# Ternary convolution after group norm: Newton step of the norm's scale on GpSimd, with the planes and copies of image 1 rearranged

## The chip, the cores and the metric

The kernel runs on one core of a Trainium2 chip. Its engines are TensorE (PE in the rows), VectorE (DVE), ScalarE (ACT), GpSimd (POOL) and SyncE (SP, which issues transfers here). The metric is the device time of the one launch, in microseconds. "Before" is the kernel as it was, "after" the changed one.

## The reference

x is 32 images of 128 channels, 56 x 56, float32. Each image is normalized in 32 groups of 4 channels, convolved 3 x 3 with ternary weights, and added to the input.

```python
def reference(x, weight, bias, Wp, Wn):
    g = x.reshape(32, 32, 4, 56, 56)
    m = mean(g, axis=(2, 3, 4)); s = var(g, axis=(2, 3, 4))
    xn = ((g - m) / sqrt(s + 1e-5)).reshape(x.shape)
    w = weight / max(abs(weight)); delta = 0.05 * max(abs(w))
    tern = where(w > delta, 1, where(w < -delta, -1, 0))
    wq = where(tern > 0, Wp * tern, where(tern < 0, Wn * tern, tern))
    return x + conv3x3(xn, wq, padding=1) + bias
```

## The kernel before

**Data.** Channels lie on the 128 partitions, and one image is one unit of work. The rows of an image are taken in pairs: two output rows are made from four products instead of six, so each image has four "planes" of 28 x 56 sums and differences of input rows, called C, D, A and B (`plane[j]`). A plane is scaled by `norm_scale` (256 over the standard deviation) and cut into a float16 high part and a float16 low part (`parts`). TensorE multiplies both parts with the three columns of the turned weights: `multiply`, 24 matmuls for each plane, 96 for an image. Products C and A go to the even output rows' PSUM tile, D and B to the odd rows'.

**Slots.** Each engine runs its own program and follows the same sequence of slots (`slots`): in one slot it works on images `prev`, `now`, `nxt` and `far` (the images k-1, k, k+1, k+2). Slots at both ends are written out, those between run in a loop of four. The engines are tied only by semaphores. What an engine does in a slot, and in which order, is its `emit`. There are 33 slots; the first has no `now`, in the second `now` is image 0, in the third `now` is image 1.

**One ordinary slot.** VectorE makes the low part of D (`make_lo`, L607), reads the variance of the next image out of PSUM (`variance`, L585), makes the low part of A, plane C of the next image (`make_c`, L561), its plane D (`make_d`, L567), then the reciprocal of its standard deviation (`first_rstd`, L591) and two more tiny instructions for the scale (`newton_factor`, L596, and `scale_of_x`, L602, one Newton step on the rough root), the low part of B, the next plane A (`make_a`, L573) and the next low part of C, and last evicts four half images of output rows out of PSUM (`output_rows`, L622). ScalarE makes the high parts (`make_hi`, L388), copies the finished products C and D out of PSUM with the bias (`copy_c`, L373, `copy_d`, L379), takes the square root (`root`, L440), and sums x and its squares two images ahead (L394, L434). GpSimd makes the next plane B (`difference_b`, L326), which waits for `lo_ready[C]` of the same image, and issues the two transfers that add the residual x to the output (`add_residual`, L339). SyncE loads images and stores outputs; each image has one of four buffers.

**TensorE's order in a slot** is product C, the group sum of squares of `nxt` (`sum_var`, L757, two tiny float32 matmuls), product D, product A, the group sum of `far` (`sum_mean`, L752), product B. Product C waits for `lo_ready[C]` and for the first half of the previous image's even rows; product D waits for `lo_ready[D]`; A for `lo_ready[A]` and `c_ready`; B for `lo_ready[B]` and `d_ready`.

**The scale's way.** `sumsq_ready` -> `sum_var` -> `variance` -> `root` (ScalarE) -> `first_rstd` -> Newton step -> `scale_of_x_ready`, for which ScalarE's `make_hi(nxt, C)` waits, and VectorE's `make_lo(nxt, C)` waits for that.

Of the kernel before, what the change touches and what calls it, by code (L numbers as in the profile page):

```python
# [6 lines left out]
P = 128  # L7
# [23 lines left out]
def conv_preact_kernel(nc, x, weight, bias, wp, wn, out):  # L31
# [15 lines left out]
    with ExitStack() as ctx:  # L47
        def sb(name, shape, dt=F32):
            return ctx.enter_context(nc.sbuf_tensor(name, shape, dt))
# [38 lines left out]
        rstd0 = sb("rstd0", [P, X_BUFS])  # L88
        newton = sb("newton", [P, X_BUFS])
        norm_scale = sb("norm_scale", [P, X_BUFS])  # L90
# [44 lines left out]
        newton_ready = sem("newton_ready")  # L135
# [164 lines left out]
        def _(pool):  # L300
# [19 lines left out]
            def run(p):  # L320
                def difference_b(img):
                    pool.wait_ge(x_loaded[img.buf], img.turn * 32 + 32)
                    wait(pool, lo_ready[B], img.count())
                    pool.wait_ge(lo_ready[C], img.count(plus=1))
                    even = x_sb[img.buf][:, 0:H:2, :]
                    nc.gpsimd.tensor_tensor(plane[B][:, 0:PAIRS - 1, :], even[:, 0:PAIRS - 1, :], even[:, 1:, :],  # L326
                                            ALU.subtract).then_inc(plane_ready[B], 1)
# [13 lines left out]
                def emit(prev, now, nxt, far):  # L341
                    if now and nxt:
                        difference_b(nxt)
                    if now and nxt:
                        add_residual(now, 0)
                        add_residual(now, 1)

                slots(p, pool, emit)

            run(0)  # L350
# [6 lines left out]
        def _(act):  # L357
# [8 lines left out]
            def run(p):  # L366
# [76 lines left out]
                def emit(prev, now, nxt, far):  # L443
# [20 lines left out]
                    elif now:  # L464
                        make_hi(now, A)
                        make_hi(now, B)
                        copy_c(now)
                        if nxt:
                            root(nxt)
                        if far:  # L470
                            sum_x(far)
                        copy_d(now)
                        if nxt:
                            make_hi(nxt, C)
# [22 lines left out]
        def _(dve):  # L497
            nc.vector.memset(no_bias[:], 0.0).then_inc(zero_ready, 1)
# [46 lines left out]
            def run(p):  # L545
# [47 lines left out]
                def newton_factor(img):  # L593
                    b = b_slice(img)
                    dve.wait_ge(rstd_ready, img.count(plus=1))
                    nc.vector.tensor_scalar(newton[:, b], rstd0[:, b], rstd0[:, b], neg_var[:, b],  # L596
                                            ALU.mult, ALU.mult).then_inc(newton_ready, 1)

                def scale_of_x(img):
                    b = b_slice(img)  # L600
                    dve.wait_ge(newton_ready, img.count(plus=1))
                    nc.vector.tensor_scalar(norm_scale[:, b], newton[:, b], 3.0, rstd0[:, b],  # L602
                                            ALU.add, ALU.mult).then_inc(scale_of_x_ready, 1)

# [42 lines left out]
                def emit(prev, now, nxt, far):  # L647
                    first_slot, second_slot = not now and not prev, now and not prev
                    if first_slot:
# [8 lines left out]
                        newton_factor(nxt)  # L658
                        scale_of_x(nxt)
                        turned_weights((C, D))  # L660
                        make_first_lo(nxt)
                    if second_slot:
# [10 lines left out]
                        newton_factor(nxt)  # L673
                        scale_of_x(nxt)
# [3 lines left out]
                    elif now:  # L678
                        third_slot = prev.j == 0 and prev.q == p * N_IMG // X_BUFS
                        make_lo(now, D)  # L680
                        if third_slot:
                            make_a(now)
# [3 lines left out]
                        if nxt:  # L686
                            make_c(nxt)
                            make_d(nxt)
                            first_rstd(nxt)
                            newton_factor(nxt)  # L690
                            scale_of_x(nxt)
# [174 lines left out]
```

## Time and profile before

| | |
|---|---|
| time, median of 3 runs | 567.59 us (567.28 to 568.82) |
| the profiled execution's own time | 566.68 us |
| its span in the trace | 565.0 us |
| busy: PE / DVE / ACT / POOL | 531.7 / 543.4 / 504.1 / 162.6 us |
| share of the span: PE / DVE / ACT / POOL | 94% / 96% / 89% / 29% |
| granted TensorE clock, mean | 0.996 of full speed |
| bytes moved, mean rate | 153.43 MB, 272 GB/s |

How to read it: busy times are sums over one profiled execution. The span is shorter than the execution's own time by 1.7 us, which lies outside the first and last instruction. Consecutive VectorE and ScalarE instructions overlap by some 0.1 us in the records, so the price of an instruction in a full queue is the distance from its start to the next start, not its duration.

### The profile page before, as it was taken

The page shows a single profiled execution, that of the slowest core. Times are in us where ns is not written, and L with a number is a line of the kernel's source. Part 1 is how long each engine was busy: PE and PEld are TensorE (multiplying, and loading weights), DVE is VectorE, ACT ScalarE, POOL GpSimd, SP SyncE. Part 2 cuts the span into 40 slices and gives each one's busy share as a digit, 9 for nine tenths or more (in the row PEclk, how much of TensorE's full clock was granted, in tenths as well). Part 3 has the DMA queues.
Part 4 walks back from the last instruction along what each step waited for, and adds up shares of the span by engine and source line. Part 5 has one row for each costly group of instructions (what it writes and reads, how often), then busy time and mean ns, then how long its engine had stood idle before and what let it go on. Part 6 is the DMA issues. An engine that isn't in the chain of part 4 may idle for free.

```text
span 565.0 us, 9357 instructions
## 1 busy us (share of the span) xinstructions
PE 531.7 (94%) x3233; PEld 319.3 (57%) x3233; DVE 543.4 (96%) x506; ACT 504.1 (89%) x485; POOL 162.6 (29%) x106
## 2 busy tenths in 40 slices
PE   1898999999999999999999999999999999999994
PEld 0654555655555555555555555556555555555552
DVE  4998999999999999999999999999999999999994
ACT  4898999999999999999999999999999999999850
POOL 2030333311333331233332123333113333312330
PEclk9999999999999999999999999999999999999998
DMA  8439799999999999999999999999999999998767
GB/s 295 202 115 256 239 286 293 293 261 266 289 299 288 313 278 270 294 294 318 297 297 278 279 298 261 309 282 302 268 301 277 292 289 304 293 281 195 155 180 276
DMA packets 28105, 153.43 MB, mean 272 GB/s; under 512 B 3505, under 2 KB 3505, under 8 KB 28081
## 3 DMA queue, kind: packets, MB, share of 16 engines
q1 hardware_dynamic: 18576, 102.77, 48.2%
q0 software_dynamic: 8928, 49.78, 45.5%
q10 hardware_dynamic: 576, 0.59, 0.3%
q8 instruction: 12, 0.20, 0.1%
q14 instruction: 13, 0.10, 0.0%
HBM read 101.75 MB, written 51.38 MB: 271 GB/s over the span
## 4 chain that ended last, share of the span: by engine, by line
DVE 69%; issue 23%; PE 2%; ACT 2%; DMA 1%; DVEq 1%; ACTq 0%
DVE parts L607 26%; DVE y L622 19%; DVE plane L561 10%; DVE plane L567 9%; DVE newton L596 2%; PE odd_rows L766 1%; DMA x<-in_x_dram 1%; DVE plane L573 1%; PE even_rows L766 1%; DVEq L157 1%; DVE neg_var L585 1%; ACT junk L434 1%; DVE rstd L591 0%; DVE parts L613 0%; ACT junk L394 0%
## 5 line engine op out<-in xcount | busy, mean ns | idle before, releaser
L766 PE MATMUL odd_rows<-parts,w_lhsT 128*128 128x385 f16 (+1 forms) x1536 | 266.1, 330 | 7.8 <-DVE parts L607 7.5
L766 PE MATMUL even_rows<-parts,w_lhsT 128*128 128x385 f16 (+1 forms) x1536 | 265.6, 330 | 3.6 <-ACT c_sb L373 2.3
L607 DVE SCALAR_TENSOR_TENSOR parts<-plane,norm_scale,parts 128x1568 f16<-128x1568 f32 x127 | 233.5, 1843 | 1.7 <-ACT parts L388 1.7
L326 POOL TENSOR_TENSOR plane<-x 128x1512 f32<-128x1512 f32 x31 | 105.8, 3412 | 379.1 <-DVE parts L607 379.1
L766 PEld LDWEIGHTS even_rows<-parts,w_lhsT 128*128 128x128 f16 x1536 | 149.3, 98 | 110.0 <-issue 4.9
L388 ACT ACTIVATE parts<-plane,norm_scale 128x1568 f16<-128x1568 f32 x127 | 199.9, 1597 | 11.8 <-ACT plane L428 5.2
L766 PEld LDWEIGHTS odd_rows<-parts,w_lhsT 128*128 128x128 f16 x1536 | 147.9, 99 | 107.3 <-DVE parts L607 9.8
L434 ACT ACTIVATE junk<-x,negmean 128x3136 f16<-128x3136 f32 x32 | 92.9, 2904 | 0.1
L394 ACT ACTIVATE junk<-x 128x3136 f16<-128x3136 f32 x31 | 86.9, 2804 | 0.0
L622 DVE SCALAR_TENSOR_TENSOR y<-even_rows,out_scale,d_sb 128x784 f32<-128x784 f32 x62 | 61.0, 1026 | 0.0
L622 DVE SCALAR_TENSOR_TENSOR y<-odd_rows,out_scale,c_sb 128x784 f32<-128x784 f32 x62 | 60.9, 1024 | 0.0
L561 DVE SCALAR_TENSOR_TENSOR plane<-x,neg2mean 128x1568 f32<-128x1568 f32 x32 | 59.0, 1845 | 0.0
L567 DVE TENSOR_TENSOR plane<-x 128x1568 f32<-128x1568 f32 x32 | 57.1, 1784 | 0.4 <-ACT junk L402 0.4
L379 ACT ACTIVATE d_sb<-odd_rows,bias_sb,out_scale 128x1568 f32<-128x1568 f32 x32 | 52.6, 1643 | 5.3 <-PE odd_rows L766 5.3
L573 DVE TENSOR_TENSOR plane<-x 128x1512 f32<-128x1512 f32 x32 | 55.2, 1725 | 0.0
L339 POOL DMA_DIRECT2D y<-in_x_dram x62 | 54.3, 887 | 3.2 <-DVE y L622 0.5
L373 ACT ACTIVATE c_sb<-even_rows,bias_sb,out_scale 128x1568 f32<-128x1568 f32 x32 | 52.5, 1641 | 0.5 <-DVE out_scale L543 0.4
L419 ACT ACTIVATE neg2mean<-odd_rows 128x1 f32<-128x1 f32 x32 | 5.4, 170 | 22.7 <-PE odd_rows L752 21.6
L757 PEld LDWEIGHTS odd_rows<-sums,group_mean 128*128 128x128 f32 x64 | 11.6, 194 | 5.6 <-issue 3.5
L752 PEld LDWEIGHTS odd_rows<-sums,group_mean 128*128 128x128 f32 x62 | 11.2, 195 | 3.4 <-DVE parts L607 0.9
L757 PE MATMUL odd_rows<-sums,group_mean 128*128 128x1 f32 x64 | 9.2, 213 | 3.4 <-ACT junk L434 3.4
L427 ACT ACTIVATE plane<-x,negmean 128x56 f32<-128x56 f32 x32 | 10.6, 332 | 0.0
(65 smaller groups left out, 109.9 us busy)
## 6 DMA issues: line engine op xcount, KB each, us to landing
x<-in_x_dram SPq DMA_DIRECT2D x64, 784.0 KB, 11.0
out_dram<-y SPq DMA_DIRECT2D x63, 784.0 KB, 5.6
y<-in_x_dram POOLq DMA_DIRECT2D x62, 784.0 KB, 11.9
out_dram<-y SPq DMA_DIRECT2D x2, 392.0 KB, 5.9
y<-in_L_conv_weight_dram ACTq DMA_DIRECT2D x1, 576.0 KB, 6.7
wp_sb<-in_L_conv_Wp_dram ACTq DMA_DIRECT2D x1, 0.5 KB, 7.7
wn_sb<-in_L_conv_Wn_dram ACTq DMA_DIRECT2D x1, 0.5 KB, 7.9
bias_sb<-in_L_conv_bias_dram ACTq DMA_DIRECT2D x1, 0.5 KB, 7.6
```

The source lines that it names most:

```text
L326: nc.gpsimd.tensor_tensor(plane[B][:, 0:PAIRS - 1, :], even[:, 0:PAIRS - 1, :], even[:, 1:, :], ALU.subtract).then_inc(plane_ready[B], 1)
L339: pool.dma_start(y, of, accum_op=ALU.add).then_inc(residual_added[img.buf][h], 16)
L379: nc.scalar.activation(d_sb[:], product_ps(ODD), ACT.Identity, bias=(no_bias if p else bias_sb)[:, 0:1], scale=out_scale[:, p, 1:2]).then_ ...
L388: nc.scalar.activation(part(img, j, HI), plane[j][:], ACT.Copy, scale=norm_scale[:, b_slice(img)]).then_inc(hi_ready[j], 1)
L394: nc.scalar.activation(junk[:], x_sb[img.buf][:].rearrange("p h w -> p (h w)"), ACT.Copy, accum_out=sums[:, img.buf, 1:2]).then_inc(sum_re ...
L434: nc.scalar.activation(junk[:], x_sb[img.buf][:].rearrange("p h w -> p (h w)"), ACT.Square, bias=negmean[:, b_slice(img)], accum_out=sums[ ...
L561: nc.vector.scalar_tensor_tensor(plane[C][:], xs[:, 0:H:2, :], neg2mean[:, b_slice(img)], xs[:, 1:H:2, :], ALU.add, ALU.add).then_inc(plan ...
L567: nc.vector.tensor_tensor(plane[D][:], xs[:, 1:H:2, :], xs[:, 0:H:2, :], ALU.subtract).then_inc(plane_ready[D], 1)
L573: nc.vector.tensor_tensor(plane[A][:, 1:, :], odd[:, 1:, :], odd[:, 0:PAIRS - 1, :], ALU.subtract).then_inc(plane_ready[A], 1)
L607: nc.vector.scalar_tensor_tensor(part(img, j, LO), plane[j][:], norm_scale[:, b_slice(img)], part(img, j, HI), ALU.mult, ALU.subtract).the ...
L622: nc.vector.scalar_tensor_tensor(rows_of(y_sb[img.buf], h, odd), product_ps(odd, 2 * h, 2 * h + 2), out_scale[:, p, 0:1], other[:, 2 * h:2 ...
L766: ins = nc.tensor.matmul(product_ps(odd, b, b + 1)[:, 0, :, to:to + n], w_lhsT[:, prod, kw, :], part(img, prod, which)[:, b * BANK_ROWS:(b ...
```

## The change

Three things. (1) VectorE loses `newton_factor` and `scale_of_x`; GpSimd does the same arithmetic in four instructions on 128 x 1 values, each waiting for the one before by a semaphore: square, times `neg_var`, plus three, times `rstd0`. It does so at the head of its slot, ahead of plane B and of the residual transfers. In VectorE's ordinary slots the reciprocal moves from behind `make_d` to ahead of it. (2) In the second slot GpSimd makes plane A of image 1 (`second_a`), ahead of plane B; VectorE no longer makes it in the third slot. (3) In the third slot ScalarE copies c ahead of the high parts of A and B instead of behind them. A tile `three` is filled once by VectorE. The diff runs through GpSimd's program first, then ScalarE's, then VectorE's.

```diff
+            def run(p):
+                def scale_of_x(img):
+                    b = b_slice(img)
+                    pool.wait_ge(rstd_ready, img.count(plus=1))
+                    nc.gpsimd.tensor_tensor(rstd_sq[:, b], rstd0[:, b], rstd0[:, b], ALU.mult).then_inc(newton_step, 1)
+                    pool.wait_ge(newton_step, img.count(3, 1))
+                    nc.gpsimd.tensor_tensor(less[:, b], rstd_sq[:, b], neg_var[:, b], ALU.mult).then_inc(newton_step, 1)
+                    pool.wait_ge(newton_step, img.count(3, 2))
+                    nc.gpsimd.tensor_tensor(newton[:, b], less[:, b], three[:], ALU.add).then_inc(newton_step, 1)
+                    pool.wait_ge(newton_step, img.count(3, 3))
+                    nc.gpsimd.tensor_tensor(norm_scale[:, b], newton[:, b], rstd0[:, b],
+                                            ALU.mult).then_inc(scale_of_x_ready, 1)
+                def second_a(img):
+                    pool.wait_ge(x_loaded[img.buf], img.turn * 32 + 32)
+                    wait(pool, lo_ready[A], img.count())
+                    odd = x_sb[img.buf][:, 1:H:2, :]
+                    nc.gpsimd.tensor_tensor(plane[A][:, 1:, :], odd[:, 1:, :], odd[:, 0:PAIRS - 1, :],
+                                            ALU.subtract).then_inc(plane_ready[A], 1)
...
                 def emit(prev, now, nxt, far):
+                    if nxt:
+                        scale_of_x(nxt)
+                    if now and not prev:
+                        second_a(nxt)
                     if now and nxt:
                         difference_b(nxt)
                     if now and nxt:
                         add_residual(now, 0)
                         add_residual(now, 1)
...
+            pool.wait_ge(zero_ready, 1)
             run(0)
...
                     elif now:
-                        make_hi(now, A)
-                        make_hi(now, B)
-                        copy_c(now)
+                        if prev.j == 0 and prev.q == p * N_IMG // X_BUFS:
+                            copy_c(now)
+                            make_hi(now, A)
+                            make_hi(now, B)
+                        else:
+                            make_hi(now, A)
+                            make_hi(now, B)
+                            copy_c(now)
...
+            nc.vector.memset(three[:], 3.0)
...
                     elif now:
-                        third_slot = prev.j == 0 and prev.q == p * N_IMG // X_BUFS
                         make_lo(now, D)
-                        if third_slot:
-                            make_a(now)
                         if nxt:
                             variance(nxt)
                         make_lo(now, A)
                         if nxt:
                             make_c(nxt)
+                            first_rstd(nxt)
                             make_d(nxt)
-                            first_rstd(nxt)
-                            newton_factor(nxt)
-                            scale_of_x(nxt)
                         make_lo(now, B)
```

In the first two slots VectorE's two calls go too, and its reciprocal stays where it was.

**VectorE, one ordinary slot.** The kernel before, from the low part of D to the first evictions (line numbers of before):

```order
L607 SCALAR_TENSOR_TENSOR parts<-plane,norm_scale,parts 128x1568
L585 TENSOR_SCALAR neg_var<-odd_rows 128x1
L607 SCALAR_TENSOR_TENSOR parts<-plane,norm_scale,parts 128x1568
L561 SCALAR_TENSOR_TENSOR plane<-x,neg2mean 128x1568
L567 TENSOR_TENSOR plane<-x 128x1568
L591 RECIPROCAL rstd<-std 128x1
L596 TENSOR_SCALAR newton<-rstd,neg_var 128x1
L602 TENSOR_SCALAR norm_scale<-newton,rstd 128x1
L607 SCALAR_TENSOR_TENSOR parts<-plane,norm_scale,parts 128x1568
L573 TENSOR_TENSOR plane<-x 128x1512
L607 SCALAR_TENSOR_TENSOR parts<-plane,norm_scale,parts 128x1568
L622 SCALAR_TENSOR_TENSOR y<-even_rows,out_scale,d_sb 128x14x56 x2
```

And the changed kernel at the same place (line numbers of after):

```order
L630 SCALAR_TENSOR_TENSOR parts<-plane,norm_scale,parts 128x1568
L620 TENSOR_SCALAR neg_var<-odd_rows 128x1
L630 SCALAR_TENSOR_TENSOR parts<-plane,norm_scale,parts 128x1568
L596 SCALAR_TENSOR_TENSOR plane<-x,neg2mean 128x1568
L626 RECIPROCAL rstd<-std 128x1
L602 TENSOR_TENSOR plane<-x 128x1568
L630 SCALAR_TENSOR_TENSOR parts<-plane,norm_scale,parts 128x1568
L608 TENSOR_TENSOR plane<-x 128x1512
L630 SCALAR_TENSOR_TENSOR parts<-plane,norm_scale,parts 128x1568
L645 SCALAR_TENSOR_TENSOR y<-even_rows,out_scale,d_sb 128x14x56 x2
```

The two tiny instructions are gone, and the reciprocal stands one large instruction earlier: three large ones (plane D, low part of B, plane A) now lie between it and the next low part of C.

**GpSimd, from the constants to the end of the second slot.** Before, after the constants (`turn`) the first work is plane B of image 1:

```order
L310 AFFINE_SELECT ident<-ident 128x128
L313 AFFINE_SELECT group_mean<-group_mean 128x128
L317 AFFINE_SELECT turn<-turn 128x128 x3
L326 TENSOR_TENSOR plane<-x 128x1512
L339 DMA y<-in_x_dram 128x1568 x2
```

In the changed kernel, for image 1 (the four tiny ones for image 0 stand once more ahead of these):

```order
L328 TENSOR_TENSOR rstd_sq<-rstd 128x1
L330 TENSOR_TENSOR less<-rstd_sq,neg_var 128x1
L332 TENSOR_TENSOR newton<-less,three 128x1
L334 TENSOR_TENSOR norm_scale<-newton,rstd 128x1
L342 TENSOR_TENSOR plane<-x 128x1512
L350 TENSOR_TENSOR plane<-x 128x1512
L363 DMA y<-in_x_dram 128x1568 x2
```

Each later slot has the same rows without L342, so plane B and the residual's transfers now stand behind four tiny instructions that wait for VectorE's reciprocal.

**ScalarE, third slot.** Before (the row at L388 is the high parts of A and B, L373 the copy of c):

```order
L388 ACTIVATE parts<-plane,norm_scale 128x1568 x2
L373 ACTIVATE c_sb<-even_rows,bias_sb,out_scale 128x1568
L440 ACTIVATE std<-neg_var 128x1
L394 ACTIVATE junk,sums<-x 128x3136
L379 ACTIVATE d_sb<-odd_rows,bias_sb,out_scale 128x1568
```

The changed kernel there:

```order
L402 ACTIVATE c_sb<-even_rows,bias_sb,out_scale 128x1568
L417 ACTIVATE parts<-plane,norm_scale 128x1568 x2
L469 ACTIVATE std<-neg_var 128x1
L423 ACTIVATE junk,sums<-x 128x3136
L408 ACTIVATE d_sb<-odd_rows,bias_sb,out_scale 128x1568
```

Only the copy of c moved, ahead of the two high parts; the later slots keep the old order.

## Rows read from the trace of the kernel before

**Rows 1.** The page's busy table: busy us, share of the span, instructions.

```profile
PE 531.7 (94%) x3233; PEld 319.3 (57%) x3233; DVE 543.4 (96%) x506; ACT 504.1 (89%) x485; POOL 162.6 (29%) x106
```

**Rows 2.** Timeline, VectorE, one slot: start us, duration us, line, operation.

```profile
260.97 1.84 DVE L607 SCALAR_TENSOR_TENSOR parts<-plane,norm_scale,parts 128x1568 f16<-128x1568 f32 x1
262.73 0.15 DVE L585 TENSOR_SCALAR neg_var<-odd_rows 128x1 f32<-128x1 f32 x1
262.80 1.84 DVE L607 SCALAR_TENSOR_TENSOR parts<-plane,norm_scale,parts 128x1568 f16<-128x1568 f32 x1
264.56 1.84 DVE L561 SCALAR_TENSOR_TENSOR plane<-x,neg2mean 128x1568 f32<-128x1568 f32 x1
266.32 1.78 DVE L567 TENSOR_TENSOR plane<-x 128x1568 f32<-128x1568 f32 x1
268.02 0.15 DVE L591 RECIPROCAL rstd<-std 128x1 f32<-128x1 f32 x1
268.22 0.27 DVE L596 TENSOR_SCALAR newton<-rstd,neg_var 128x1 f32<-128x1 f32 x1
268.52 0.21 DVE L602 TENSOR_SCALAR norm_scale<-newton,rstd 128x1 f32<-128x1 f32 x1
268.65 1.84 DVE L607 SCALAR_TENSOR_TENSOR parts<-plane,norm_scale,parts 128x1568 f16<-128x1568 f32 x1
270.41 1.73 DVE L573 TENSOR_TENSOR plane<-x 128x1512 f32<-128x1512 f32 x1
272.06 1.84 DVE L607 SCALAR_TENSOR_TENSOR parts<-plane,norm_scale,parts 128x1568 f16<-128x1568 f32 x1
```

**Rows 3.** Chain that ended last: first and last plane C of the ordinary slots.

```profile
65.16 1.85 DVE plane L561
...
530.43 1.85 DVE plane L561
```

**Rows 4.** Timeline, TensorE, the same slot; [idle before <-releaser].

```profile
258.36 4.15 PE L766 MATMUL even_rows<-parts,w_lhsT 128*128 128x392 f16 x24
262.35 0.28 PE L757 MATMUL odd_rows<-sums,group_mean 128*128 128x1 f32 x2
262.87 4.16 PE L766 MATMUL odd_rows<-parts,w_lhsT 128*128 128x392 f16 x24 [0.24 <-DVE parts L607]
266.87 4.15 PE L766 MATMUL even_rows<-parts,w_lhsT 128*128 128x392 f16 x24
270.86 0.28 PE L752 MATMUL odd_rows<-sums,group_mean 128*128 128x1 f32 x2
271.00 4.15 PE L766 MATMUL odd_rows<-parts,w_lhsT 128*128 128x392 f16 x24
```

**Rows 5.** Timeline, ScalarE, same slot: next high part of C, next mean.

```profile
268.86 1.59 ACT L388 ACTIVATE parts<-plane,norm_scale 128x1568 f16<-128x1568 f32 x1
271.17 0.17 ACT L419 ACTIVATE neg2mean<-odd_rows 128x1 f32<-128x1 f32 x1 [0.72 <-PE odd_rows L752]
```

**Rows 6.** GpSimd's groups by form: count, busy us, mean ns, idle before.

```profile
L326 POOL TENSOR_TENSOR plane<-x 128x1512 f32<-128x1512 f32 x31 | 105.8, 3412 | 379.1 <-DVE parts L607 379.1
...
L308 POOL TENSOR_SCALAR_AFFINE_SELECT group_mean<-group_mean 128x128 f32<-128x128 f32 x1 | 0.5, 518 | 0.1
...
L855 POOL MEMSET const-float32-0.0<- 128x1 f32 x1 | 0.1, 98 | 0.4 <-issue 0.4
```

**Rows 7.** Timeline, the first and the third slot, ScalarE, TensorE and VectorE.

```profile
19.20 1.77 ACT L413 ACTIVATE parts<-plane,norm_scale 128x784 f16<-128x784 f32 x2
...
43.37 0.28 PE L757 MATMUL odd_rows<-sums,group_mean 128*128 128x1 f32 x2
...
45.13 3.10 ACT L388 ACTIVATE parts<-plane,norm_scale 128x1568 f16<-128x1568 f32 x2 [1.98 <-DVE plane L573]
46.77 1.85 DVE L607 SCALAR_TENSOR_TENSOR parts<-plane,norm_scale,parts 128x1568 f16<-128x1568 f32 x1 [1.65 <-ACT parts L388]
```

**Rows 8.** The page's DMA issues: count, KB each, median us to landing.

```profile
x<-in_x_dram SPq DMA_DIRECT2D x64, 784.0 KB, 11.0
```

More of the change, by code:

```diff
@@ L88, in conv_preact_kernel @@
         rstd0 = sb("rstd0", [P, X_BUFS])
+        rstd_sq = sb("rstd_sq", [P, X_BUFS])
+        less = sb("less", [P, X_BUFS])
         newton = sb("newton", [P, X_BUFS])
+        three = sb("three", [P, 1])
         norm_scale = sb("norm_scale", [P, X_BUFS])
@@ L134, in conv_preact_kernel @@
         rstd_ready = sem("rstd_ready")
-        newton_ready = sem("newton_ready")
+        newton_step = sem("newton_step")
         scale_of_x_ready = sem("scale_of_x_ready")
@@ L591, in first_rstd @@
                     nc.vector.reciprocal(rstd0[:, b], std[:, b]).then_inc(rstd_ready, 1)
[L593 to L603, printed above, removed]
                 def make_lo(img, j):
@@ L672, in emit @@
                         first_rstd(nxt)
-                        newton_factor(nxt)
-                        scale_of_x(nxt)
                         make_lo(now, B)
@@ L687, in emit @@
                             make_c(nxt)
+                            first_rstd(nxt)
                             make_d(nxt)
-                            first_rstd(nxt)
-                            newton_factor(nxt)
-                            scale_of_x(nxt)
                         make_lo(now, B)
```

## The prediction

> **What bounds the kernel now.** I read the busy table first: VectorE is at 96% [rows 1]. That is an average, so I then read the chain that ended last, which is a string of VectorE instructions, one image after another: plane C starts at 65.16 and, 28 slots on, at 530.43 [rows 3], so a slot takes 465.27 / 28 = 16.617 us. The timeline of one slot shows why: VectorE's starts follow each other with no gap [rows 2]. TensorE is close behind. Product C starts at 258.36, the sum of squares at 262.35 (3.99 later), product D at 262.87, A at 266.87, the group sum at 270.86 and B at 271.00 [rows 4]. A group sum that nobody holds up costs 0.14 (270.86 to 271.00); the one before D costs 0.52, because D waits for its low part. So TensorE loses only 0.38 us in a slot, and could do one in 16.617 - 0.38 = 16.24. ScalarE waits 0.72 for the next mean [rows 5], so it isn't the bound either. GpSimd makes one plane in 3.41 us and is idle for 379.1 us in all [rows 6].
>
> **VectorE's part of the change.** From the reciprocal's start to the next large instruction are 268.65 - 268.02 = 0.63 us [rows 2]. A tiny instruction that nothing waits on costs about 0.07 (262.73 to 262.80, the variance), so the reciprocal alone will cost 0.07, and each slot gets 0.56 us shorter on VectorE: 16.06. The root must be there earlier now, at plane C's end (266.32). It is made from the variance at 262.73, and ScalarE has it well before its copy of d and the high part at 268.86; I charge nothing.
>
> **What stops TensorE next.** VectorE cannot simply run at 16.06, and the slot does not fall to 16.24 either. VectorE takes the variance only after TensorE's sum of squares: 0.28 us after its start (its duration) at least, 0.38 at most (262.35 to 262.73) [rows 2, 4]; I take 0.33. From there VectorE needs a slot of its own, 16.06, plus 0.08 for the end of the next low part of D (260.97 + 1.84 = 262.81 against 262.73), and 0.06 to release product D: D starts 16.53 after the previous sum of squares. From D's start to the next sum of squares TensorE needs 4.00 + 3.99 + 0.14 + 3.98 + 3.99 = 16.10. This chain (sum of squares, VectorE's slot, product D, TensorE's slot) spans two images: 32.63 / 2 = 16.31 us (16.29 to 16.34 with 0.28 and 0.38). It is longer than TensorE's own 16.24 and VectorE's own 16.06, so it is the new bound: 0.307 saved in each of 28 slots, **8.6 us**.
>
> **GpSimd's chain.** The trace of before has no tiny two-input instruction on GpSimd. Bounds from its rows: not less than the 0.10 of a 128 x 1 fill, and hardly more than the 0.52 of a select over 128 x 128 floats [rows 6]; with some 0.1 for each semaphore hand-over the four cost 0.8 to 2.5 us. I take 0.2 + 0.1 each, 1.2 us in all, nearer to the fill because the size is the fill's. The cover: the reciprocal will end 0.15 after plane C, the low part of C starts after plane D, the low part of B and plane A, 1.70 + 1.76 + 1.65 = 5.11 less 0.08, and ScalarE's high part must lie before it (1.59, and 0.05 for the hand-over): **3.4 us** are free [rows 2, 5]. Against ScalarE's own time the cover is also enough at 1.2: in before's clock the reciprocal ends near 266.5 and the scale is there at 267.7, ScalarE comes at 268.86. If that cover fails, every further microsecond falls on VectorE's low part of C in each slot. Queued behind the four on GpSimd are plane B, which waits for that low part anyway, and the residual's two transfers, issued after the evictions: nothing later for them. Their head start on the next reciprocal is several us.
>
> **Transfers.** Loads take 11.0 us to land [rows 8] and are issued four images ahead into the freed buffer, over 30 us before their first reader; the whole saving over all slots, about 10 us, is less than that slack, so even a transfer rate that cannot grow costs nothing.
>
> **The edges.** Third slot: ScalarE is free at 45.13 - 1.98 = 43.15 and waits for VectorE's plane A; VectorE then waits 1.65 for the high part until 46.77 [rows 7]. After the change plane A comes from GpSimd in the second slot. If GpSimd starts it behind its tiny chain at about 33 it ends at 36.7, and plane B, released near 37.2 by the low part of C, at 40.7, both before 43.15. ScalarE copies c when product C is done (43.37), for 1.54, makes the high part of A from 44.96 to 46.55, and VectorE's low part starts at 46.6 instead of 46.77: only 0.1, since the copy now stands in front; with the 0.56 of this slot 0.7. What TensorE gains earlier in that slot is lost again, because its next product C waits for VectorE's evictions. Second slot: VectorE gains 0.56, but the next image's sum of x on ScalarE sets the slot, so nothing. First slot: the scale comes 0.70 us after the reciprocal's start now and 0.15 + 1.2 = 1.35 then; ScalarE starts its first high part at 19.20 without a wait, so between 0 and 0.65 is lost; I take 0.1. Last slots: the last pass through VectorE's chain once more, 0.56 less what it now waits, about 0.4.
>
> **The sum**, against the profiled execution's own 566.68: 8.6 + 0.7 + 0.4 - 0.1 = 9.6, so 557.1. The median of the runs shown is 0.9 higher, so I forecast **558.0 us**.
>
> **Rivals.**
> (a) *GpSimd and VectorE take turns, and the scale comes late: slower.* All of VectorE's large instructions behind the reciprocal read two SBUF tensors, and so do the new GpSimd ones. In before no such pair ever overlaps: plane B waits for the low part of C in all 31 cases (379.1 us of idle time) and lies beside the evictions, which read PSUM and one SBUF tensor [rows 6]. So the trace neither shows nor excludes it. If a GpSimd instruction has to wait for the end of VectorE's current one, the first gets in behind plane D, the second behind the low part of B, the third behind plane A, and the fourth when VectorE stands at the low part of C. Then 0.3 for the fourth, 1.64 for the high part: VectorE waits about 2.0 in each slot, and each of the first three lets it wait some 0.1 more. 16.06 + 2.0 + 0.3 = 18.4, 1.75 more than now, times 29 slots is +51: **about 618 us** (610 to 628). It decides from the point where the chain of four takes over 3.4 + 0.56 = 4.0 us: then VectorE waits at the low part of C for as long as it saved. For it speaks that the wait on the low part of C is no data dependence, which leaves plane B clear of exactly these instructions; against it, that reading a value of 128 x 1 is over at once, so that the gap of some 0.1 between two large instructions may do. The Trainium skill (SBUF — State Buffer, Who interferes with whom) says that a VectorE instruction with two SBUF inputs contends with a GpSimd instruction that reads SBUF, and that the side that comes first holds the shared ports. By that rule the time would be that of this rival; no run here shows it yet. Chance 0.17.
> (b) *The same contention, but mild:* GpSimd's instructions slip in, and each holds VectorE for 0.1 to 0.15. Four give VectorE's slot 16.06 + 0.4 to 0.6, that is 16.46 to 16.66, against 16.617 now: 561.5 to 568.5. Chance 0.12.
> (c) *No gain:* TensorE or ScalarE turns out to run no faster than 16.6 for a reason that its idle time hides. Against it, TensorE has the 0.38 and ScalarE 0.72. 566 to 569. Chance 0.06.
> (d) *A GpSimd instruction of this form simply takes over 0.9 us*, without any contention; the chain, with 0.1 for each hand-over, then passes 4.0 us. At 1.2 each it is 4.8, and the slot 16.06 + 1.4 = 17.5, +24: 592. All rows of small GpSimd work stand at 0.1 to 0.5 against it. Chance 0.03.
> The forecast itself (chain hidden, new bound at 16.31): 0.62.
>
> **How the numbers follow.** Low end: TensorE at its own 16.24 would save 0.38 x 28 = 10.6 instead of 8.6, and the edges up to 0.7 more, which is 555.3; 554.5 with the spread of runs. High end: (b) and (c), 568.5. What lies outside is (a) and (d), 0.20. A measurement of this kernel tells 0.3%, 1.7 us, from no change. Faster: the forecast 0.62 and less than half of (b), 0.05, in all 0.67. Same: (c) 0.06 and most of the rest of (b), 0.07, together 0.13. Slower: 0.20.
>
> **What would show it.** Right: plane C to plane C 16.31 on average, with alternating long and short slots possible; a wait of VectorE for the sum of squares at the variance (0.1 to 0.3) where none was; TensorE's wait at D down from 0.24; GpSimd's four instructions done within 1.2 us of the reciprocal, and no wait of ScalarE for the scale; in the third slot the low part of A released at 46.6. Wrong: tiny GpSimd instructions that start only where a large VectorE instruction ends; ScalarE's high part of C waiting for GpSimd, and VectorE's low part of C for ScalarE; large VectorE instructions with gaps of 0.1 and more between their starts.

## The result, and the profile after

The changed kernel takes **628.14 us** (median of 4 runs, 627.01 to 630.18), before 567.43 (4 runs): ratio 1.107, interval 1.105 to 1.110. It is 60.7 us slower. The forecast was 558.0; rival (a), that GpSimd and VectorE take turns and the scale comes late, had been given 618 and a chance of 0.17.

The busy table of the page, after, against [rows 1]:

```profile
PE 541.1 (86%) x3233; PEld 317.3 (51%) x3233; DVE 530.5 (85%) x442; ACT 503.6 (80%) x485; POOL 331.4 (53%) x235
```

Nobody is at 96% any more: VectorE lost 13 us of work and is now idle for 96 us of 626, and GpSimd doubled its busy time, though it got only 128 instructions on 128 x 1 values and one plane. Its groups say which (count, busy us, mean ns; behind the second bar the idle time before them and what ended it), to be read against [rows 6]:

```profile
L350 POOL TENSOR_TENSOR plane<-x 128x1512 f32<-128x1512 f32 x31 | 105.8, 3413 | 112.8 <-DVE parts L630 112.8
L330 POOL TENSOR_TENSOR less<-rstd_sq,neg_var 128x1 f32<-128x1 f32 x32 | 100.1, 3130 | 2.5
...
L328 POOL TENSOR_TENSOR rstd_sq<-rstd 128x1 f32<-128x1 f32 x32 | 53.3, 1665 | 152.6 <-DVE rstd L626 152.6
L334 POOL TENSOR_TENSOR norm_scale<-newton,rstd 128x1 f32<-128x1 f32 x32 | 6.1, 189 | 2.5
L332 POOL TENSOR_TENSOR newton<-less,three 128x1 f32<-128x1 f32 x32 | 6.1, 189 | 2.5
```

Four instructions of one form and one size take 1665, 3130, 189 and 189 ns on average. The size can't be the reason; what stands beside them can. The timeline of the changed kernel (start us, duration us, engine, line; in brackets the idle time before and what ended it), first in the opening slots, then in one ordinary slot:

```profile
17.95 1.00 DVE L586 CAST w_lhsT<-even_rows 128x384 f16<-128x384 f32 x2
18.18 0.19 POOL L328 TENSOR_TENSOR rstd_sq<-rstd 128x1 f32<-128x1 f32 x1 [14.49 <-DVE rstd L626]
...
21.38 5.87 PE L780 MATMUL even_rows<-parts,w_lhsT 128*128 128x392 f16 x24 [0.65 <-DVE parts L636]
...
33.52 3.43 POOL L328 TENSOR_TENSOR rstd_sq<-rstd 128x1 f32<-128x1 f32 x1 [14.33 <-DVE rstd L626]
...
37.70 3.40 POOL L342 TENSOR_TENSOR plane<-x 128x1512 f32<-128x1512 f32 x1
...
39.42 3.33 DVE L630 SCALAR_TENSOR_TENSOR parts<-plane,norm_scale,parts 128x1568 f16<-128x1568 f32 x1 [2.53 <-ACT parts L417]
...
45.08 5.98 PE L780 MATMUL even_rows<-parts,w_lhsT 128*128 128x392 f16 x24
...
54.42 1.85 DVE L630 SCALAR_TENSOR_TENSOR parts<-plane,norm_scale,parts 128x1568 f16<-128x1568 f32 x1 [3.04 <-ACT parts L417]
...
278.76 0.16 DVE L626 RECIPROCAL rstd<-std 128x1 f32<-128x1 f32 x1
278.83 1.77 DVE L602 TENSOR_TENSOR plane<-x 128x1568 f32<-128x1568 f32 x1
279.00 1.66 POOL L328 TENSOR_TENSOR rstd_sq<-rstd 128x1 f32<-128x1 f32 x1 [3.93 <-DVE rstd L626]
...
280.52 1.85 DVE L630 SCALAR_TENSOR_TENSOR parts<-plane,norm_scale,parts 128x1568 f16<-128x1568 f32 x1
280.74 3.33 POOL L330 TENSOR_TENSOR less<-rstd_sq,neg_var 128x1 f32<-128x1 f32 x1
282.28 1.73 DVE L608 TENSOR_TENSOR plane<-x 128x1512 f32<-128x1512 f32 x1
...
284.14 0.19 POOL L332 TENSOR_TENSOR newton<-less,three 128x1 f32<-128x1 f32 x1
284.41 0.19 POOL L334 TENSOR_TENSOR norm_scale<-newton,rstd 128x1 f32<-128x1 f32 x1
284.63 1.60 ACT L417 ACTIVATE parts<-plane,norm_scale 128x1568 f16<-128x1568 f32 x1 [2.58 <-POOL norm_scale L334]
...
286.26 1.85 DVE L630 SCALAR_TENSOR_TENSOR parts<-plane,norm_scale,parts 128x1568 f16<-128x1568 f32 x1 [2.25 <-ACT parts L417]
```

Read it by where things end. In the ordinary slot plane D ends at 278.83 + 1.77 = 280.60, and GpSimd's first tiny instruction at 280.66. Plane A ends at 284.01, the second tiny one at 284.07. Once VectorE has run out of work, the third and fourth take 0.19 each, 0.27 from start to start. Then ScalarE makes the high part, and VectorE, which stood at the low part of C since about 283.92, starts it at 286.26: 2.3 us lost in each slot. VectorE's own instructions are not stretched: from plane D to the low part of B it takes 1.69 and on to plane A 1.76, as in [rows 2] (1.70 with the reciprocal behind it, and 1.76). At 18.18, beside a VectorE instruction that reads PSUM, the same GpSimd instruction takes 0.19.

Where the 61.6 us between the two profiled executions (628.3 and 566.68) lie:

| stretch | before | after | more |
|---|---|---|---|
| start to the fourth plane C, the first counted in [rows 3] | 65.16 | 74.58 | 9.4 |
| 28 slots, plane C to plane C | 465.27 (16.617 each) | 515.11 (18.397 each) | 49.8 |
| last plane C to the end of the span | 34.57 | 36.51 | 1.9 |
| outside the span | 1.7 | 2.1 | 0.4 |

### The profile page after: what moved, and what is told of

Read it like the earlier page. It is cut to its first block, busy times and chain, and to the rows that moved or that the text cites. A ratio compares the mean times of both kernels' runs of the same rounds, so it can differ in the third digit from the quotient of the medians.

```text
span 626.2 us, 9501 instructions
## 1 busy us (share of the span) xinstructions
PE 541.1 (86%) x3233; PEld 317.3 (51%) x3233; DVE 530.5 (85%) x442; ACT 503.6 (80%) x485; POOL 331.4 (53%) x235
## 4 chain that ended last, share of the span: by engine, by line
POOL 40%; issue 25%; DVE 16%; ACT 10%; PE 5%; POOLq 2%; DMA 1%; DVEq 0%; ACTq 0%
POOL less L330 16%; DVE parts L630 10%; POOL plane L350 10%; POOL rstd_sq L328 8%; ACT parts L417 8%; DVE y L645 4%; POOL y L363 4%; PE even_rows L780 2%; PE odd_rows L780 2%; DMA x<-in_x_dram 1%; POOL newton L332 1%; POOL norm_scale L334 1%; DVE plane L596 1%; ACT junk L423 1%; POOLq L363 0%
## 5 line engine op out<-in xcount | busy, mean ns | idle before, releaser
L780 PE MATMUL even_rows<-parts,w_lhsT 128*128 128x385 f16 (+1 forms) x1536 | 269.4, 333 | 49.0 <-DVE y L645 46.8
L417 ACT ACTIVATE parts<-plane,norm_scale 128x1568 f16<-128x1568 f32 x127 | 200.0, 1598 | 90.4 <-POOL norm_scale L334 82.4
L780 PEld LDWEIGHTS odd_rows<-parts,w_lhsT 128*128 128x128 f16 x1536 | 146.0, 100 | 112.1 <-DVE parts L630 11.1
L328 POOL TENSOR_TENSOR rstd_sq<-rstd 128x1 f32<-128x1 f32 x32 | 53.3, 1665 | 152.6 <-DVE rstd L626 152.6
L330 POOL TENSOR_TENSOR less<-rstd_sq,neg_var 128x1 f32<-128x1 f32 x32 | 100.1, 3130 | 2.5
L608 DVE TENSOR_TENSOR plane<-x 128x1512 f32<-128x1512 f32 x31 | 53.7, 1732 | 0.0
```

What stands on the lines that cost most here:

```text
L328: nc.gpsimd.tensor_tensor(rstd_sq[:, b], rstd0[:, b], rstd0[:, b], ALU.mult).then_inc(newton_step, 1)
L330: nc.gpsimd.tensor_tensor(less[:, b], rstd_sq[:, b], neg_var[:, b], ALU.mult).then_inc(newton_step, 1)
L417: nc.scalar.activation(part(img, j, HI), plane[j][:], ACT.Copy, scale=norm_scale[:, b_slice(img)]).then_inc(hi_ready[j], 1)
L780: ins = nc.tensor.matmul(product_ps(odd, b, b + 1)[:, 0, :, to:to + n], w_lhsT[:, prod, kw, :], part(img, prod, which)[:, b * BANK_ROWS:(b ...
```

## The experiments

Nine more kernels ran. Most of them test a theory T against a rival R. Theory T: while VectorE runs an instruction with two SBUF inputs, a GpSimd instruction that reads SBUF waits. Rival R: the long tiny instructions are slow for reasons of their own (their operands, their place, the other two parts of the change).

**e1, the Newton step alone.** In the changed kernel `second_a` goes, VectorE's third slot makes plane A again, and the copy of c goes back:

```diff
-                    if now and not prev:
-                        second_a(nxt)
...
+                        if third_slot:
+                            make_a(now)
```

> Only the Newton step on GpSimd; plane A of image 1 and the copy of c as before. Theory T (GpSimd waits for VectorE's two-SBUF-input instructions): the ordinary slot stays at 18.4 us with the same two long tiny instructions (1.7 and 3.3 us), and only the third slot and the second differ from the changed kernel: 616 to 624 us, since in the changed kernel plane A on GpSimd also held VectorE's low part of C for some 1.5 us. Rival R (the long slot comes from the interplay with the other two parts, or the slow start): below 600. The first two slots tell whether TensorE's late rise to 2.4 GHz belongs to the Newton step.

624.85 us, ratio 1.101 (1.099 to 1.104). Slot (585.43 - 70.38) / 28 = 18.395, the two long instructions at 1665 and 3129 ns on average. So the Newton step carries 57.3 of the 60.7 us. The time is 0.9 us above the range that I gave.

**e2, the other two parts alone.** The kernel before, with plane A of image 1 on GpSimd and the copy of c first in the third slot.

> Only plane A of image 1 on GpSimd and the copy of c first; the Newton step on VectorE as before. Ordinary slots must stay at 16.62. Theory T: GpSimd's 3.4 us instruction asks for the ports during plane C of image 1, gets them behind it and then holds VectorE's next two-input instruction for up to 3.4 us; the third slot gives back 0.1 to 0.7. Net +0 to +3 us, 567.5 to 571. Rival R (no exclusion): the third slot's gain alone, -0.2 to -1, 566.5 to 567.2.

570.25 us, ratio 1.004 (1.003 to 1.006): 2.7 us slower, in T's range. Its ordinary slots stay at (535.02 - 69.75) / 28 = 16.617. The timeline shows both directions of the exclusion in the second slot, and two rows of the third:

```profile
30.75 1.83 DVE L575 SCALAR_TENSOR_TENSOR plane<-x,neg2mean 128x1568 f32<-128x1568 f32 x1
...
30.98 4.88 POOL L325 TENSOR_TENSOR plane<-x 128x1512 f32<-128x1512 f32 x1 [27.28 <-DVE parts L621]
...
33.13 4.38 DVE L621 SCALAR_TENSOR_TENSOR parts<-plane,norm_scale,parts 128x1568 f16<-128x1568 f32 x1
...
48.18 1.66 ACT L382 ACTIVATE c_sb<-even_rows,bias_sb,out_scale 128x1568 f32<-128x1568 f32 x1 [0.55 <-PE even_rows L777]
...
51.36 1.85 DVE L621 SCALAR_TENSOR_TENSOR parts<-plane,norm_scale,parts 128x1568 f16<-128x1568 f32 x1 [3.05 <-ACT parts L397]
```

GpSimd's plane takes 3.41 alone. Here it is asked for 0.23 after VectorE's plane C starts and ends at 35.86, 4.88 later: it waited until about 32.45. VectorE's low part of B, 1.84 long, then takes 4.38, since it waits for GpSimd until 35.86. The three tiny VectorE instructions between them, with one SBUF tensor and pointer scalars (a value per partition, read through a pointer), run beside GpSimd's plane at their usual 0.14, 0.27 and 0.21. The third slot gives nothing back; why stands further down.

**e3, which border lets GpSimd in.** As e1, with plane A directly behind plane D:

```diff
                             make_d(nxt)
+                            make_a(nxt)
                         make_lo(now, B)
                         if nxt:
-                            make_a(nxt)
                             make_lo(nxt, C)
```

> As the Newton-only kernel, but in ordinary slots VectorE makes planes D and A one behind the other and the low part of B after them. Theory T says which borders let GpSimd in. If it gets in behind a tensor_tensor (whatever follows): the first tiny instruction takes 1.7 us (end of plane D), the second 1.6 to 1.7 (end of plane A), the third 1.8 (held by the low part of B), the fourth 0.19; slot about as before, 18.4. If it gets in only ahead of an instruction with a pointer scalar: the first takes 3.3 us (end of plane A), the second 1.7 (end of the low part of B), the last two 0.19. Rival R (the 3.3 us belongs to the second instruction itself, its operands or its place in the chain): 1.7 and 3.3 as before, whatever the order.

One run, 624.36 us. Its timeline in an ordinary slot:

```profile
274.32 1.77 DVE L595 TENSOR_TENSOR plane<-x 128x1568 f32<-128x1568 f32 x1
274.49 3.30 POOL L328 TENSOR_TENSOR rstd_sq<-rstd 128x1 f32<-128x1 f32 x1 [3.93 <-DVE rstd L619]
...
276.02 1.73 DVE L601 TENSOR_TENSOR plane<-x 128x1512 f32<-128x1512 f32 x1
277.66 1.84 DVE L623 SCALAR_TENSOR_TENSOR parts<-plane,norm_scale,parts 128x1568 f16<-128x1568 f32 x1
277.87 1.68 POOL L330 TENSOR_TENSOR less<-rstd_sq,neg_var 128x1 f32<-128x1 f32 x1
```

The long one is now the first instruction, not the second, so R falls in so far as it lays the 3.3 us on the second instruction: the price goes with VectorE's order. The border from plane D to plane A was closed, plane A to the low part of B open (277.79 against plane A's end at 277.75). That is the second of T's two cases.

**e4, no second input.** As e1, but planes D and A and the low part of B are made by instructions of the same size with one SBUF input, which changes what they compute:

```diff
+                def one_input(out, of, done):
+                    nc.vector.tensor_reduce(out, of.unsqueeze(3), AX_X, ALU.max).then_inc(done, 1)
```

> As the Newton-only kernel, but in ordinary slots VectorE's three large instructions behind the reciprocal read one SBUF tensor each: reductions over an axis of length one, of the same size, instead of the differences for planes D and A and of the low part of B. This replaces part of the computation, so only its times are read. Theory T: nothing holds GpSimd, its four instructions take 0.19 each, 1.0 us in all, ScalarE doesn't wait for the scale, and the slot is 16.2 to 16.6, depending on what the reductions take, so 555 to 570. Rival R (GpSimd is slow for reasons of its own, or by any VectorE instruction beside it): the 1.7 and 3.3 us stay and the slot is 18.4, some 620.

One run, 559.76 us. Its timeline, and then three of its waits (us in total, times, longest):

```profile
282.05 1.77 DVE L634 TENSOR_REDUCE plane<-x 128x1568 f32<-128x1568 f32 x1
...
282.22 0.19 POOL L328 TENSOR_TENSOR rstd_sq<-rstd 128x1 f32<-128x1 f32 x1 [4.26 <-DVE rstd L619]
282.48 0.19 POOL L330 TENSOR_TENSOR less<-rstd_sq,neg_var 128x1 f32<-128x1 f32 x1
...
283.02 0.19 POOL L334 TENSOR_TENSOR norm_scale<-newton,rstd 128x1 f32<-128x1 f32 x1
...
284.49 1.59 ACT L415 ACTIVATE parts<-plane,norm_scale 128x1568 f16<-128x1568 f32 x1
```

```profile
ACT neg2mean L446 <- PE odd_rows L779: 11.9, 28, 0.7
...
DVE neg_var L613 <- PE odd_rows L784: 8.1, 30, 1.6
...
ACT parts L415 <- POOL norm_scale L334: 3.1, 1, 3.1
```

With VectorE just as full, but with one input, the chain takes 283.21 - 282.22 = 0.99 us, ScalarE comes later than the scale, and waits for it once, in the second slot, which this edit leaves as it was, instead of 31 times and 82.4 us in the changed kernel. The slot is (524.08 - 68.54) / 28 = 16.269, and VectorE now waits for the sum of squares in 30 slots. This settles T against R. That it is the second SBUF input, and not the operation, is seen from the evictions: they are `scalar_tensor_tensor` too, with one input in PSUM and one in SBUF, and GpSimd's plane B takes its 3.41 beside them.

**e5, a pointer scalar behind the closed border.** As e1, with plane A made by the same arithmetic with a pointer scalar:

```diff
+                    nc.vector.scalar_tensor_tensor(plane[A][:, 1:, :], odd[:, 1:, :], one[:], odd[:, 0:PAIRS - 1, :],
+                                                   ALU.mult, ALU.subtract).then_inc(plane_ready[A], 1)
```

> As the Newton-only kernel, but in ordinary slots VectorE makes plane A with a scalar_tensor_tensor whose pointer scalar is a column of ones: same result, same two SBUF inputs, now with a pointer scalar. Theory P (GpSimd gets the ports only ahead of a VectorE instruction with a pointer scalar, or when VectorE stands still): the second tiny instruction now ends with the low part of B, 1.6 instead of 3.3 us, the third is held by plane A, 1.6 instead of 0.19, the fourth takes 0.19; the slot stays 18.4 and the time 622 to 627. Rival Q (the border behind the low part of B is closed for another reason, for example what stands ahead of it): 1.7, 3.3, 0.19, 0.19 as before.

One run, 618.38 us (lower than the range given; its slot is (580.02 - 70.79) / 28 = 18.187). The timeline:

```profile
274.59 1.68 POOL L331 TENSOR_TENSOR less<-rstd_sq,neg_var 128x1 f32<-128x1 f32 x1
276.14 1.79 DVE L609 SCALAR_TENSOR_TENSOR plane<-x,one 128x1512 f32<-128x1512 f32 x1
276.35 1.63 POOL L333 TENSOR_TENSOR newton<-less,three 128x1 f32<-128x1 f32 x1
...
278.05 0.19 POOL L335 TENSOR_TENSOR norm_scale<-newton,rstd 128x1 f32<-128x1 f32 x1
```

Now the second instruction ends with the low part of B (276.27) and the third with plane A (277.98), as theory P has it. The border opened when the instruction behind it became a `scalar_tensor_tensor` with a pointer scalar; which of the two opens it, the form or the pointer, no run separates. The chain ends 0.2 us sooner, as only one tiny instruction is left behind plane A, and the slot is 0.2 shorter.

**e6 and e7, other places for the same work.** Both are edits of the kernel before. e6 keeps all on VectorE and moves plane D between the Newton factor and the scale. e7 puts the last step on ScalarE, with the constants folded into the variance and the root, and the factor behind plane D. The two main places of e7:

```diff
+                            first_rstd(nxt)
                             make_d(nxt)
-                            first_rstd(nxt)
                             newton_factor(nxt)
-                            scale_of_x(nxt)
...
+                    nc.scalar.activation(norm_scale[:, b], newton[:, b], ACT.Identity, bias=rstd0[:, b],
+                                         scale=rstd0[:, b]).then_inc(scale_of_x_ready, 1)
```

> The kernel before with the three tiny instructions spread on VectorE: reciprocal and Newton factor behind plane C, plane D, then the scale. The chain's waits on itself shrink from 0.63 to 0.20 + 0.07 + 0.07 = 0.34 us, VectorE's own slot is 16.33, and the two-image loop of the prediction gives (16.33 + 0.47 + 16.10) / 2 = 16.45. If the loop theory holds: 0.17 x 28 = 4.7 us faster, 562 to 564. If VectorE alone sets the slot: 16.33, 0.29 x 28 = 8, 559 to 560. If TensorE's or ScalarE's floor is higher than thought: 567.

> The last tiny step on ScalarE instead of GpSimd (one activation, newton times reciprocal plus reciprocal, with the constants folded into the variance and the root), the Newton factor on VectorE behind plane D, the reciprocal ahead of it. VectorE pays 0.07 twice, its own slot is 16.13, the loop 16.35; ScalarE gets about 0.2 for the activation and 0.2 for waiting on it, out of the 0.7 us that it is idle. If ScalarE has that room: 16.35 to 16.4, 559 to 561. If ScalarE becomes the bound (its 0.72 less 0.4 less the 0.27 by which the slot shrinks leaves 0.05): up to 16.5, 563 to 565.

e6: 564.44 us, ratio 0.995 (0.994 to 0.997), 0.4 above the 562 to 564 expected. e7: **560.60 us, ratio 0.988 (0.986 to 0.990)**, in its range and faster than before and after. e6's timeline, then e7's, show what the tiny instructions really cost:

```profile
264.97 0.16 DVE L591 RECIPROCAL rstd<-std 128x1 f32<-128x1 f32 x1
265.16 0.27 DVE L596 TENSOR_SCALAR newton<-rstd,neg_var 128x1 f32<-128x1 f32 x1
265.35 1.78 DVE L567 TENSOR_TENSOR plane<-x 128x1568 f32<-128x1568 f32 x1
...
267.05 0.21 DVE L602 TENSOR_SCALAR norm_scale<-newton,rstd 128x1 f32<-128x1 f32 x1
267.17 1.84 DVE L607 SCALAR_TENSOR_TENSOR parts<-plane,norm_scale,parts 128x1568 f16<-128x1568 f32 x1
```

```profile
266.11 0.27 DVE L605 TENSOR_SCALAR newton<-rstd,neg_var 128x1 f32<-128x1 f32 x1
266.30 1.84 DVE L610 SCALAR_TENSOR_TENSOR parts<-plane,norm_scale,parts 128x1568 f16<-128x1568 f32 x1
266.87 0.38 ACT L419 ACTIVATE norm_scale<-newton,rstd 128x1 f32<-128x1 f32 x1
267.27 1.60 ACT L388 ACTIVATE parts<-plane,norm_scale 128x1568 f16<-128x1568 f32 x1
```

The factor, with two pointer scalars, costs 0.19 and not 0.07; the scale, with one, 0.12. So e6 saves 0.13 and not 0.29: VectorE's own slot is 16.49, the two-image loop (16.49 + 0.47 + 16.10) / 2 = 16.53, and measured is 16.523. e7 saves 0.37: own slot 16.25, loop 16.41, measured 16.394. ScalarE pays 0.40 for its step and still has the room.

**e8 and e9, one pointer scalar.** e8 is e7 with the factor as one `scalar_tensor_tensor`, which has one pointer scalar; e9 is e7 again beside it.

> The kernel with the last step on ScalarE, and the Newton factor as a scalar_tensor_tensor with one pointer scalar instead of a tensor_scalar with two. In that kernel the factor cost VectorE 0.19, where the scale with one pointer scalar costs 0.12 and the reciprocal with none 0.07 (starts to next starts). If the price goes by the number of pointer scalars: 0.12, VectorE's own slot 16.18, the loop (16.18 + 0.47 + 16.10) / 2 = 16.37 against 16.39, about 1 us less, 559.5 to 560.3. If it goes by something else, 0.19 and no difference, 560.6.

> The kernel with the last step on ScalarE once more, on the same chip as the one with a single pointer scalar, so that the two can be compared: 560.3 to 561, slot 16.39.

e8: 560.45 us, ratio 0.987 (0.985 to 0.989), between the two times expected; e9: 560.41, ratio 0.988 (0.986 to 0.990), in its range. The timeline of e8 has 0.13 for the factor instead of 0.19 (267.17 to 267.30), and the slots are 16.371 against e9's 16.395, near the 16.37 and 16.39 expected. The 0.7 us over all slots is lost in the spread of the runs, so this stays without a measured gain in time.

```profile
267.17 0.21 DVE L605 SCALAR_TENSOR_TENSOR newton<-rstd,neg_var 128x1 f32<-128x1 f32 x1
267.30 1.84 DVE L610 SCALAR_TENSOR_TENSOR parts<-plane,norm_scale,parts 128x1568 f16<-128x1568 f32 x1
```

## Why the prediction was wrong

**The step that failed** is the one headed "GpSimd's chain". It priced the four at "0.2 + 0.1 each, 1.2 us in all", and said that "3.4 us are free". The cover was right. The price holds for a GpSimd with nothing in its way: 0.99 us in e4, and what was put at nothing is the wait for VectorE's instructions. In the changed kernel the chain takes 284.60 - 279.00 = 5.6 us from its start, and 5.7 from the reciprocal's end, well past the 4.0 us from which rival (a) "decides". That gives VectorE's own 16.06 + 5.7 - 3.4 = 18.4, and 18.397 was measured. The rows that carried the price, a fill and a select [rows 6], had run while VectorE had nothing with two SBUF inputs to do, so they could not bound it from above. I saw that no such pair overlaps in the trace of before and took that as no evidence either way; but an instruction that waits for what its data don't need, in 31 of 31 cases, is a reason to price the pair as exclusive until a run shows otherwise. Two of the three signs of being wrong came (tiny instructions that end with large ones, and both waits for the high part of C); the third, gaps between large VectorE instructions, did not.

The Trainium skill (SBUF — State Buffer, Who interferes with whom) says that the side that comes first holds the shared ports and the other is blocked. The runs agree that one side is blocked: 0.19 against 1.66 and 3.33 for a GpSimd instruction, and 4.38 against 1.84 for a VectorE one in e2. In who comes first they differ at the closed border: the second tiny instruction had been waiting since 280.74, and plane A, which starts at 282.28, still went ahead of it. Here the measurement decides.

**Rival (a)** had the slot right, 18.4, by two errors that cancel. It let one tiny instruction in at the end of each of three large ones, and charged VectorE 0.1 for each. In fact the border between the low part of B and plane A is closed, so the second instruction waits for two large ones, two tiny ones are left instead of one when VectorE stands still (0.3 more), and VectorE is not held up by them at all (0.3 less). Its total of 618 is 10 short because it took all else at no cost: 7.6 in the opening slots beyond the 1.8 of the third, which it had counted, and 2.3 at the end. Its reason, that the two engines take turns, was right; that its slot came out to 0.1 us was luck.

**The opening slots**, forecast as 0.7 less 0.1 of gain, cost 9.4, of which 1.8 is the third slot's share of the full price. For the second slot the prediction said that ScalarE's sum of x sets it, "so nothing". But the high part of C stands ahead of that sum on ScalarE. The first tiny instruction ends after 3.43, with plane D; the high part of C starts at 37.78 instead of 33.22, the sum of x at 39.29 instead of 34.71, and TensorE's group sum waits 3.42 for it. The low part of C starts 3.4 later than in before (39.42 against 36.02), and then takes 3.33 instead of 1.85, because GpSimd's plane A runs from 37.70 to 41.10. TensorE's next product C, 4.15 in before, takes 5.98. The low part of C in before:

```profile
36.02 1.85 DVE L607 SCALAR_TENSOR_TENSOR parts<-plane,norm_scale,parts 128x1568 f16<-128x1568 f32 x1
```

TensorE's wait in the changed kernel, and a stretch of it (start and end; length; busy us of PE, PEld, DVE, ACT and POOL; granted clock, DMA share, GB/s):

```profile
42.24 0.58 PE L766 MATMUL odd_rows<-sums,group_mean 128*128 128x1 f32 x2 [3.42 <-ACT junk L423]
...
44.00:50.00 6.00, 6.00 (x23) 2.96 (x22) 4.28 (x4) 3.93 (x5) 4.18 (x3) 0.60 0.36 46
```

Taken 2 us at a time, the granted clock is 0.99 from 40 to 42, 0.50, that is 1.2 GHz, from 42 to 48, and 0.80 from 48 to 50. It fell when TensorE had stood idle for those 3.42 us. Before kept 1.00 there. Either part of the change alone brings such a fall, though a shorter one: e1 has 0.50 from 42 to 44 after TensorE stood idle for 3.43, e2 has 0.54 and 0.60 from 38 to 42 after 2.52. Product C of image 0 also took longer, 5.87 at 21.38, which moved the variance by 1.35, though the clock reads 1.00 there; in e1, with the same first slot, it took 4.15 and the variance moved by 0.3 (0.6 in e2). So this is no sure part of the change, and its cause stays open.

**The third slot** was forecast to gain 0.7, and lost. From its low part of D to its plane C it takes 6.97 us in before (41.56 to 48.53) and in e1 (45.01 to 51.98), but 8.12 in e2 (45.01 to 53.13) and 9.75 in the changed kernel (46.44 to 56.19). The prediction had product C done at 43.37, when ScalarE was free at 43.15. In e2 ScalarE ends its other work at 47.63, and GpSimd's plane A has been there since 35.86, but the copy in front waits for product C until 48.18. The high part of A then starts at 49.74, and VectorE waits 3.05 for it. In the old order it could have started 2.1 earlier: an estimate from these rows, since the copy's place was not tried by itself. So plane A on GpSimd costs in the second slot, and the copy's place most likely in the third.

The low end of the range has a small slip: it counts the edges as 0.7 in all, where the sum has 1.0. Nothing rests on it.

**What held.** VectorE's saving, 0.56 in each slot, and its own 16.06: the measured 18.397 less the 2.34 for which it stands at the low part of C (283.92 to 286.26). In the first slot ScalarE starts its high part at 19.22 instead of 19.20. The loop of two images, "16.31 us (16.29 to 16.34)", was not seen in the changed kernel, which has another bound. With VectorE's own slot taken from their rows it gives 16.53, 16.41 and 16.38 for e6, e7 and e8 and 16.27 for e4 (the reductions are 0.10 shorter in all, own slot 15.96), and measured are 16.523, 16.394, 16.371 and 16.269. In e7, e8 and e9 that is 0.13 to 0.15 above what VectorE (16.25, 16.19) or TensorE (16.24) needs by itself, and the loop can be seen: e7's slots alternate between 16.24 and 16.55, VectorE's variance waits 0.23 for the sum of squares in every second one, and TensorE's product D 0.18 for its low part in every second one. In e4 and e6 one engine alone would give nearly the same (16.24, 16.49), so they don't tell. That transfers are hidden also held: e4 and e7 run 7.8 and 6.4 us faster than before with all of them.

e1 and e2 add up to the change: 57.3 + 2.7 = 60.0 of 60.7 us.

## What to carry to other kernels

Price an instruction that moves to GpSimd by what VectorE runs beside it, not by its size: beside VectorE instructions with two SBUF inputs it runs when they let it, and a chain of small ones can pay at each link: here four took 5.6 us instead of 1.0. If the chain feeds the engine that is full, what exceeds its cover (3.4 us here) comes back in each slot. Look for slack on ScalarE first: here one step there, and the rest spread between large instructions, brought 1.2%.

When the engine that is busiest gets shorter, look for the loop that crosses two engines over two iterations: in e7, e8 and e9 it was 0.13 to 0.15 us longer than either engine's own slot, and it set the time.

## What the runs showed of the hardware

- A GpSimd `tensor_tensor` on 128 x 1 takes 0.19 us, and 0.27 from start to start in a dependent chain, when no VectorE instruction with two SBUF inputs runs (the changed kernel at 18.18 and 284.14, e4).
- Between two back-to-back VectorE instructions with two SBUF inputs, GpSimd got in where the second was a `scalar_tensor_tensor` with a pointer scalar (plane D to low part of B, plane A to low part of B, low part of B to plane A in e5), and not where it was a plain `tensor_tensor` (low part of B to plane A or D, plane D to plane A). When it got in, VectorE's next start was not later (1.69 behind plane D, against 1.70). Whether the form or the pointer opens the border, and why, was not measured.
- It works in both directions: a 3.41 us GpSimd plane made a 1.84 us VectorE instruction last 4.38 (e2). VectorE instructions on 128 x 1 with one SBUF tensor, pointer scalars or not, ran beside such a plane unchanged.
- On 128 x 1, the VectorE instructions tried cost 0.07 us with no pointer scalar (reciprocal, variance), 0.12 and 0.13 with one (scale, e8's factor) and 0.19 with two (factor), from start to next start, when nothing waits on them.
